# A planned mix of attention, recurrence and experts on one core: order by the longest way to the end, and constant matmuls in planned gaps

## What is computed

```python
x = x + attn_a(layernorm(x))   # q, k, v, a gate; out += g_j * h * sum(q * shift(k)) * shift(v) over 11 scales x 4 taps
x = x + ffn(layernorm(x))      # 8 experts, each token goes to the argmax of its gate logits; gelu(x W1 + b1) W2 + b2
x = x + attn_b(layernorm(x))   # h = tanh(h A^T + x_t B^T), 512 steps in series; y = h C^T; layer norm, gamma, beta
x = x + ffn(layernorm(x))      # the same experts again
```

## Time and profile before

| | us |
|---|---|
| median of 3 runs | 1432.24 |
| lowest, highest | 1431.16, 1438.38 |
| span of the profiled execution | 1436.4 |

### The profile page before, as it was taken

How to read it: one execution, slowest core, us unless ns; L and a number is a source line. 1 busy time by engine, 2 the same in 40 slices (tenths; PEclk the granted TensorE clock), 3 DMA queues, 4 the chain that set the end, 5 groups by cost and what they waited for, 6 DMA issues and landing times. The chain is left out here.

```text
span 1436.4 us, 32831 instructions
## 1 busy us (share of the span) xinstructions
PE 1170.8 (82%) x9942; PEld 881.1 (61%) x9942; DVE 796.3 (55%) x1723; ACT 651.3 (45%) x2050; POOL 788.6 (55%) x1274
## 2 busy tenths in 40 slices
PE   3877886888888899789988899887899998995580
PEld 2644554566565666466655666676787777785570
DVE  4878788889966777576788647542122301240110
ACT  2233332465544664455554436363564344562250
POOL 2645458563776748862748844876315642324504
PEclk9989987999988998889999759788995567998895
DMA  4700001221221212111112221233332324444542
GB/s 126 213 1 0 1 1 47 61 65 58 86 66 44 64 44 70 51 51 38 44 46 86 60 63 46 77 97 105 108 104 77 98 83 123 118 132 121 146 116 60
DMA packets 117638, 107.58 MB, mean 75 GB/s; under 512 B 15540, under 2 KB 88541, under 8 KB 117469
## 3 DMA queue, kind: packets, MB, share of 16 engines
q1 hardware_dynamic: 106704, 88.01, 21.5%
q0 software_dynamic: 8192, 16.79, 3.9%
q10 hardware_dynamic: 2573, 0.69, 0.2%
HBM read 76.73 MB, written 28.70 MB: 73 GB/s over the span
## 5 line engine op out<-in xcount | busy, mean ns | idle before, releaser
L799 POOL TENSOR_TENSOR acc<-acc,term 128x512 f32<-128x512 f32 x219 | 281.5, 1286 | 71.9 <-DVE term L1341 54.8
L1160 PE MATMUL bank<-w,hT 128*128 x1088 | 217.5, 324 | 22.1 <-ACT hT L985 13.9
L1341 DVE TENSOR_TENSOR term<-bank,V 128x512 f32<-128x512 f32 x251 | 168.0, 684 | 67.2 <-PE bank L1110 44.0
L1005 ACT ACTIVATE hid<-bank 128x16 f32<-128x16 f32 x512 | 93.0, 182 | 243.6 <-PE bank L1187 203.0
L985 ACT ACTIVATE hT<-bank,b1T 128x128 f32<-128x128 f32 x544 | 165.2, 370 | 79.2 <-PE bank L1147 65.2
L839 POOL DMA_INDIRECT back<-sorted_y,slot_i x128 | 125.1, 978 | 135.8 <-DMA back<-sorted_y,slot_i 44.2
L1160 PEld LDWEIGHTS bank<-w,hT 128*128 128x128 f32 x1088 | 173.9, 221 | 41.1 <-issue 35.6
L1187 PEld LDWEIGHTS bank<-hid,abcT 128*32 128x32 f32 x4096 | 88.6, 116 | 162.2 <-ACT hid L1005 83.2
L1312 DVE SCALAR_TENSOR_TENSOR made<-bank,qkvb,K 128x512 f32<-128x512 f32 x251 | 176.2, 742 | 17.8 <-PE bank L1083 7.2
L1187 PE MATMUL bank<-hid,abcT 128*32 128x16 f32 x4096 | 138.6, 201 | 38.3 <-ACT hid L1005 37.1
L1147 PE MATMUL bank<-xTb,w1b 128*128 128x128 f32 x864 | 166.8, 321 | 3.2 <-ACT xTb L973 3.0
(11 more groups left out here) (177 smaller groups left out, 2153.4 us busy)
## 6 DMA issues: line engine op xcount, KB each, us to landing
w1b<-in_W SPq DMA_DIRECT2D x130, 256.0 KB
K<-in_W SPq DMA_DIRECT2D x54, 256.0 KB
xsb<-sorted_x SPq DMA_DIRECT2D x184, 64.0 KB
sorted_y<-ysb SPq DMA_DIRECT2D x136, 64.0 KB
X<-in_x SPq DMA_DIRECT2D x64, 64.0 KB
out_x<-X SPq DMA_DIRECT2D x64, 64.0 KB
sorted_x<-K SPq DMA_DIRECT2D x14, 256.0 KB, 3.6
sorted_y<-made SPq DMA_DIRECT2D x48, 64.0 KB
```

What stands on the lines that cost most here:

```text
L799: nc.gpsimd.tensor_tensor(acc[:], acc[:] if k > 1 else term[0][:], term[k % NTERM][:], ALU.add).then_inc(S["terms_added"], 1)
L1005: nc.scalar.activation(hid[n % 2][:, cs], bank[6 + n % 2][:, cs], ACT.Tanh).then_inc(S["h_ready"], 1)
L1160: last = nc.tensor.matmul(bank[SLOT_BANK[place(n)]][:, 0:D], tile(hT[place(n)], c), w2[:, ds(second[n] + c * D, D)], start=(c == 0), stop= ...
L1341: V_.tensor_tensor(term[k % NTERM][:], bank[2 + k % 2][:], V[:, at:at + CW], ALU.mult).then_inc(S["terms_ready"], 1)
```

## The change

It changes the planner and the fillings; the instructions of the real work and their waits stay as they are, only their order on each engine's queue is another.

1. Each piece has two durations now, pace (how long it keeps its engine) and took (until its result is there), from a table PACE. HOP gives the time from one engine to another, LANDS that of scatters and gathers. The planner also knows when engines begin, 1.283 us for a change of ACT's table between exp and gelu, the spacing of scatters and gathers, and 0.11 us for a step that follows another kind of work on PE.
2. to_go is a piece's longest way to the end. The planner takes the engine that can act first, and there, among the pieces ready within 0.15 us, the one with the longest to_go (50 us of to_go are worth 1 us of waiting). The ranks are gone.
3. Some pieces have more predecessors, so that pieces of a series stay in order.
4. fillings() goes by streamed columns: it adds up the columns of the planned pieces in the 3.4133 us up to the end of a piece, and where they are under 3900 it fills the gap ahead of the piece, 0.11 us and 256 columns each: all that lie earlier than that stretch, and in it as many as are lacking. Gaps of any length count, a bank counts as read 0.3 us (before 1.0) after its reader, and bank 0 may be used, with a wait on its reader.

```diff
-PE_PACE = 0.93
-IDLE_US, FILL_US, FILL_SHARE, FREE_US = 0.5, 0.15, 0.65, 1.0
...
+PACE = dict(
+    counts=(0.45, 0.60), gatep=(0.87, 1.02), kproj=(0.87, 1.02), vproj=(0.87, 1.02), qproj=(0.87, 1.02), logit=(0.82, 0.97),
...
+    rows=(0.42, 0.60), rxb=(0.93, 1.06), ry=(0.92, 1.06), step=(0.18, 0.25), turn=(0.12, 0.27), xT=(0.45, 0.60),
...
+    loadw=(1.10, 3.75), loadx=(0.45, 2.25), store=(0.45, 2.25), outst=(0.62, 2.60))
+HOP = {("ACT", "PE"): 0.13, ("ACT", "DVE"): 0.03, ("PE", "ACT"): 0.05, ("PE", "DVE"): 0.04, ("DVE", "PE"): 0.06, ("DVE", "ACT"): 0.03}
...
+TABLE_US, TURN_US, LOOK_US, DAWDLE = 1.283, 0.11, 0.15, 50.0
...
+        to_go[key] = max((hop(todo, key, y) + to_go[y] for y in followers[key]), default=todo[key].took)
...
-                choice = (at, todo[key][2], ready, key)
-                if pick is None or choice[0] < pick[0] - 1e-9 or (abs(choice[0] - pick[0]) < 1e-9 and choice[1:3] < pick[1:3]):
-                    pick = choice
...
+            if r <= now + LOOK_US:
+                choice = (DAWDLE * max(0.0, r - now) - to_go[key], key)
+                if best is None or choice < best[0]:
+                    best = choice, max(r, now)
...
+SPAN_US, TARGET, FILL_US, FILL_COLS, FREE_US = 3.4133, 3900, 0.11, 256, 0.3
...
-        if best and end and BEGIN[key] - best[0] > IDLE_US:
-            out[key] = int((BEGIN[key] - best[0]) * FILL_SHARE / FILL_US), best[1], best[2]
...
+        lack = TARGET - sum(c for _, c in recent) - columns_of(*key)
+        most = int((at - since) / FILL_US)
+        if end and lack > 0 and most > 0:
+            late = sum(since + FILL_US * j > stop - SPAN_US for j in range(most))
+            times = most - late + min(late, -(-lack // FILL_COLS))
+            out[key] = times, b, x
...
-                    if reader:
+                    if reader and b == 0:
+                        pe.wait_ge(S["bank0_taken"], filled)
+                    elif reader:
```

More of the change, by code:

```diff
@@ new lines, in cost @@
+def cost(what, n, k):
+    if what in ("hidden", "result"):
+        us = 0.222 * HC / parts(n)
+        return us, us + 0.17
+    if what == "gelu":
+        us = 0.25 * HC / parts(n)
+        return us, us + 0.12
+    if what == "spread" and terms(n)[k].g not in (0, 1):
+        return 0.87, 1.02
+    if what == "spread":
+        return 0.31, 0.47
+    if what == "scale" and k == 2:
+        return 0.21, 0.31
+    if what == "xmom" and STATS_GROUP[n][1] - STATS_GROUP[n][0] == 1:
+        return 3.16, 3.17
+    return PACE[what]
@@ L192, in past, with pieces, piece @@
+def pieces():
+    todo = {}
+    def piece(engine, what, n, k, after, bank0=None):
+        todo[what, n, k] = Piece(engine, *cost(what, n, k), [x for x in after if x is not None], bank0)
     def past(what, n, k=0):
         return (what, n, k) if n >= 0 else None
-    URGENT, USUAL = 0.0, 1.0
     for i in range(CHUNKS):
@@ L282, in timeline @@
-        piece("DVE", "resid", i, 0, 0.7, USUAL, [("out", i, 0)], bank0=0)
+                piece("POOL", "add", i, j, [("term", i, j), ("add", i, j - 1) if j > 1 else None, past("out", before)])
+        piece("PE", "gatep", i, 0, [("xcopy", i, 0), past("gate", before)], bank0=1)
+        piece("ACT", "tanh", i, 0, [("gatep", i, 0)], bank0=0)
+        piece("DVE", "gate", i, 0, [("add", i, n - 1), ("tanh", i, 0)])
+        piece("PE", "out", i, 0, [("gate", i, 0)], bank0=1)
+        piece("DVE", "resid", i, 0, [("out", i, 0)], bank0=0)
@@ L430, in fillings @@
+CLOSED_BY = dict(xT="xcopy", kproj="kcopy", vproj="vcopy", logit="shift", rows="rcopy", reduce2="pack2", gatep="tanh", out="resid",
+                 pT="pcopy", plog="plg", counts="ccopy")
 def fillings():
[L433 to L434 removed]
+    out, end, recent = {}, None, []
+    last_of = {b: None for b in range(8)}
     for key in ORDER["PE"]:
         what, n, k = key
+        at, stop = BEGIN[key], BEGIN[key] + WORK[key].pace
         best = None
[L438 to L439 removed]
+        for b, x in last_of.items():
+            since = max(end or at, BEGIN[x] + WORK[x].took + FREE_US) if x else end or at
```

326 lines of the change are left out of this document (172 added, 154 removed).

## The result

The kernel after took 1493.63 us (median of 4, 1486.22 to 1510.8) beside 1434.15 us of the kernel before in the same series: a ratio of 1.0424, 95% interval 1.0348 to 1.0501. Ratios and intervals leave out executions over 1.5% above the fastest of their kernel, the medians take all, so a ratio here is not exactly the quotient of the two medians. The kernel after is slower, by about 60 us, where I had forecast 146 us less. Both results have to be explained, and what lies between them is the larger part of the story.

The account below looks back on a forecast made before the run. After 250 us PE was taken to bind, in its order and its clock. 1436.4 - 58 - 80 = 1298 us, 1289 from the other side; 1290 profiled, so 1286 us. Forecast band 1225 to 1325, outer range 1205 to 1440.

Parts of the forecast that it names:

- Part 1: The new order on all five queues, by longest way to the end: 58 us gained, from (a) to (d).
- slower rival: Recurrence: fillings in front of steps lengthen each trip by up to 0.3 us, 154 us in all; 1470 us, chance 0.14.
- the plan isn't what happens: In-order queues: a plan wrong by some per cent puts pieces behind new waits; 1392 us, chance 0.10.
- Part 2: Constant matmuls in any gap short of columns keep PE's clock up after 250 us: 80 us gained.
- (a): Attention, 72 to 250 us: POOL's gate multiply goes ahead of less urgent adds, shrinking DVE's idle; 8 us gained.
- (b): Recurrence steps: one pair of matmuls between steps instead of two, trip 0.83 to about 0.61 us; 25 us gained.
- (d): Attention beside the recurrence: its last chunk moves forward, and first holes and tail get earlier work; 11 us gained.
- (c): SP's queue at the end: output stores go behind the last job's loads; 14 us gained.
- The 157 us: After 250 us, by stage: what stretches below full clock lose, if PE were the limit every moment; half was taken.
- the first rival: PE after 250 us: clock doesn't come back, order's 58 us stay and some 15 of the 80; 1360 us, chance 0.14.
- Part 3: Plan-only costs, and a wait on bank 0's reader ahead of some fillings on PE: costed at 0.
- The signs that I named: After 250 us: clock 0.93 or more, last gate before 880, steps every 0.65 to 0.9 us, 1000 to 2500 fillings.

Follow-up runs that it names:

- series 4: Kernel before again 1426.08 us, new order with old fillings 1326.81, kernel after with two DMAs in a row 1383.88; kernel before beside them 1425.54.
- series 1: New order with old fillings 1330.92 us, without fillings 1345.56, old order with new fillings 1426.62, new costs with old choice 1363.49; kernel before beside them 1423.68.
- series 3: Kernel after unedited 1335.47 us, new order with old fillings 1314.44, without fillings 1355.05, old fillings with DMA runs of three 1343.97; kernel before 1424.45.
- after again: The kernel after, unedited, measured a second time in series 3: 1335.47 us, ratio 0.9374 to the kernel before beside it.
- series 1 and 5: New order without any filling, against the kernel before: 1345.56 us (ratio 0.9473) in the one, 1349.12 us (0.9464) in the other.

## Why the prediction was wrong, point by point

**The step that failed.** The sum priced every handover from PE at what it cost in prompt rows (the trip of a step from the earlier trace rows), and no term or rival had a signal of PE held back. Part 1 says that the change moves GpSimd's scatters and gathers, and then costs only SP's queue. The new order has 41 of them in runs of eight and more where the old one has 8 (starts at most 2 us apart), and in the series that counted PE's signals were late in them. The two traces of the kernel after differ by 151.6 us of span, more than the whole 138 us that I had forecast as the gain in Parts 1 and 2; that is what late signals and the clock that fell with them cost. The 79 us of remote waits, 44.6 of them in the two largest groups, that I could have read in the trace of before would have given me the mechanism and a rival on the other side. My sum was off too where signals are prompt, in its terms (below), but those errors were small enough to stay inside the range.

**A reading that was wrong.** The prediction says that nearly two in three of the 486 constant matmuls lie before 250 us. It is 374 of them, over three in four, so the old rule had only 112 after 250 us, where I wanted the clock back.

**The slower rival** named 1470 us and the result was 1494, but by another mechanism. With no filling ahead of steps and turns the kernel took 1487 and 1497. Its arithmetic (each trip 0.3 us longer by fillings) isn't what happened: without those fillings the ratio to the kernel before is 1.031 and 1.035, with them 1.038 to 1.042, so they cost some 10 us there, not 154. Where signals are prompt the kernel without them wasn't run; there the new rule as a whole costs 21 us against the old one.

**The rival "the plan isn't what happens"** has the right form. By the plan's own begins, the kernel after runs 15 us late at 300 us, 62 at 500, 134 at 800 and 282 at 1104; without late signals it is 16, 33, 66 and 137. I put it at 1392, 106 us over the forecast; the late signals alone were worth 158 (1494 against 1335). They are about half of what the plan doesn't know: the other 137 us by 1104 remain where signals are prompt, and what they are made of wasn't taken apart.

**Part 1 where signals are prompt.** Here the result is 1335, inside the range and 89 us under the kernel before, against my 146. The order did more than I said: with the old filling rule it is worth 93 to 110 us in four series (1330.92, 1314.44, 1326.81 and 1323.12 against 1424 to 1426), where I had 58. The old rule plans 730 fillings on the new order where it had 486 on the old one; without any filling the order is still worth 69 to 78 us in three series (1345.56, 1355.05 and 1349.12). Compared with the kernel before, the new order with old fillings (series 4) has PE idle 203 us in place of 269 and the clock at 0.92 in place of 0.862. I left the clock out of Part 1 altogether. Part of its rise is the order's own, as the lines under Part 2 show. The costs account for most of the gain: under the new filling rule, the new costs with the old choice took 1363 (series 1), with the longest way 1335 (series 3), beside 1424 and 1424 of the kernel before. What the choice by the longest way adds isn't shown, since the two are from two series and the fastest of the four executions with the old choice took 1338. The terms, by the traces of before and after again in prompt series:
- (a), 8 us forecast in the first stage: the fifth gate of attention comes at 245 in place of 238 us, so there was none; the gain begins behind it, and the ninth comes at 416 in place of 425.
- (b) and (d), 36 us together: the last gate moves from 921 to 891, the last state from 1247 to 1180. Between consecutive states within the last nine chunks of the recurrence lie 0.89 us in place of 1.30 (means). That is 67 us by the last state, 57 of them after the ninth gate; I said that I would be most wrong in (d), and was.
- (c), 14 us: from the last state to the end 153 us in place of 175, 22 us. 26 of the 64 output stores now stand ahead of the last load, where 48 did.

**Part 2, the constant matmuls: 80 us forecast, nothing gained.** On the old order the new rule is at a ratio of 1.0006, on the new order it is 21 us behind the old rule in the series that has both (1335 against 1314), and 5 to 12 behind the old rule's results in the others. The old rule's fillings together are worth 15 and 41 us there (1331 against 1346, 1314 against 1355). The accounting of the kernel after again (series 3) against the old rule (series 4), both with prompt signals: fillings 185.2 us in place of 134.9, other work of PE 30 us shorter by the clock (0.937 in place of 0.92), idle time 11 us less, so 50 - 30 - 11 = 9 us more (two traces of two series). I had written that the lower bound was below nothing and that I had no row for the half that I took. The 157 us were the price of the clock's low stretches. Here is what came back of it after 250 us, up to PE's idle tail, all with prompt signals (columns as in the earlier trace rows): the kernel before (107 fillings in this stretch), the new order without any (series 1 and 5), with the old rule (323) and with the new one (545).

```profile
250.00:1385.00 1135.00, 967.02 (x9028) 746.32 (x9027) 593.60 (x1328) 574.03 (x1919) 641.95 (x1063) 0.86 0.28 81
```
```profile
250.00:1310.00 1060.00, 914.49 (x8972) 693.18 (x8972) 595.82 (x1355) 583.34 (x1934) 651.36 (x1084) 0.90 0.30 86
250.00:1326.00 1076.00, 932.20 (x8972) 710.59 (x8972) 594.27 (x1354) 586.84 (x1934) 653.54 (x1084) 0.89 0.31 85
```
```profile
250.00:1288.00 1038.00, 930.64 (x9254) 724.20 (x9253) 579.37 (x1329) 575.00 (x1922) 636.95 (x1070) 0.94 0.31 88
250.00:1296.00 1046.00, 955.32 (x9477) 744.24 (x9475) 578.01 (x1329) 576.97 (x1922) 639.28 (x1070) 0.95 0.31 87
```

The clock rises from 0.86 to 0.89 and 0.90 by the order alone, to 0.94 with the old rule's fillings, and to 0.95 with the new rule's. So fillings do bring the clock back; but the step from 0.94 to 0.95 costs as much of PE's own time as it gives, or more. The page of the new order without any filling (series 1) shows where the order alone is not enough: the clock is low in the first quarter, where attention runs by itself, and 8 and 9 in most slices after it.

```profile
PE   3776676578887778888888899999999986997670
...
PEclk9666667599997789999988988957998996999795
```

Where signals are prompt, the first rival, that the clock doesn't come back by fillings, came nearest with 1360 us. Its term for the fillings was still too high (15 us, where the new rule gave nothing over the old), its mechanism isn't what happened, and the order made up for both.

**Part 3** held: of the idle time of PE ahead of fillings in the trace of after, 0.3 us ended with another engine's work, and 22.4 in 43 places with nothing that the profile shows ("issue"), which is not larger than the 21 of the kernel after again.

**The signs that I named.** With late signals: clock 0.91, 0.82 and 0.66 in the stages from 400, 850 and 1150 us, last gate at 960, 223 us of waiting of states. All of them read wrong. With prompt ones: 0.97, 0.87 and 0.98, so one of the three is under my 0.93; last gate at 891 where I wanted 880; from 1000 us on a step every 0.77 us, as I wanted; one output store ahead of a load in the last 80 us, where the kernel before has 12; 179 us of waiting. 995 fillings were just short of the 1000 I had put as the lower end.

**A better version.** The new order with the old filling rule was the fastest of its series in all four where it ran, 1314 to 1331 us, ahead of the kernel before each time and of the kernel after in the one series that has both. All four had prompt signals. Short DMA runs give some 30 us where signals are late and cost as much where they are prompt (1344 against 1314; with two in a row 1384 against 1335 of another series), so they insure more than they gain.

## What to carry to other kernels

Read every wait whose releaser the trace doesn't show before anything else, and see what the other queues do in those microseconds: 79 us of such waits stood in the trace of before, and where they occur the kernel after takes 12% more. Then see which engine all the waiting ones read from. Where a change moves GpSimd's indirect DMAs, count how many of them it puts in a row, and how busy PE is meant to be in those stretches. And put the two kernels of a comparison in one series together with the variants; a variant from another series can differ by 150 us for no reason of its own.

## What the runs showed of the hardware

PE's signals can be held back while GpSimd issues indirect DMAs back to back: 0.07 us from a step's matmuls to ACT's start with none or one begun in the last 4 us, 0.28 to 0.37 with two, 1.07 to 1.46 with three in the new order (medians by the count up to ACT's start), and 7.6 us in the longest stall shown. It comes in some series and not in others, on the same chip, and then for each kernel. ACT's signals to PE aren't late in the same rows: PE's next step starts 0.24 us after the state of 1200.07 does. Over the trace of the kernel after the median of this time is 0.24 us with none, one, two and three DMAs alike (61 steps ahead of which PE stood idle, 0.29 us at most). The DMA packets are no slower (GpSimd's queue 0.110 us each in the late trace of the kernel after, 0.115 in the prompt one). What holds the signal isn't shown. The Trainium skill (Perfetto Trace Analysis, section "Tensor Engine Instruction (MATMUL, LD_WEIGHTS)") says that the end of a matmul in a trace is estimated, and that the signal is pushed only when PSUM has acknowledged the writes. The trace agrees as far as it goes: PE's later matmuls start while the signal of an earlier one is out, so the lateness may lie in the array's writes, in their acknowledgement or in the signal's way, and no run here tells these apart.

There is one more difference, and it opens a rival that no run here tests. The trace has a record for each rise of a semaphore, by which an engine tells of a result. In the late trace of the kernel after, 78 of the 160 results of ACT and DVE that ended with three or more such DMAs begun in the last 4 us have no record within 0.3 us; with none it is 0 of 1973. In the prompt trace of the same kernel it is 8 of 314 and 0 of 1645, and every other trace sides with one of the two in the same way. PE went on in time all the same, so these records are missing or late while their signals were not. Whatever writes the records is thus disturbed in the same microseconds, and every time in this document is of an execution whose clock was recorded. Whether the recording only suffers from the same cause, or has a part in it, stays open.

PE fetches its instructions in packets of 16 KB: 90 of them in the kernel after and 86 before, for 23057 and 22039 records of PE, 256 to a packet (that these packets are PE's is read from this count). Moving their borders by 32 and 64 instructions left the time at 1499 and 1498 us.
